# A four-layer recurrent stack on one core: weight preparation spread behind the first 64 RNN steps, initial states through the recurrence's own matmuls, vectors loaded as rows, and a hinted loop branch

## What is computed

```python
x = x + L0(x)   # RNN:  h_t = tanh(x_t @ Wx + b + h_(t-1) @ Wh),  h_0 = cond
x = x + L1(x)   # conv with 4 taps (weights: cond), 64 states: s = decay*s + dt*softplus(..)*u ; y = tanh(..)*s ; y @ Wo
x = x + L2(x)   # LSTM: A = x_t @ Wx + b + h @ Wh (512 x 2048), h_0 = cond, c_0 = 0
def L3(x, cond, base, w1, b1, w2, b2, ln_g, ln_b):
    ae = layernorm(cond) * ln_g + ln_b            # (4, 512)
    h  = gelu(ae @ w1 + b1)                       # (4, 512)
    xw = h @ w2 + b2                              # (4, 8192), w2 is 512 x 8192 (16 MB)
    x_a, x_b = split(xw)                          # each (4, 512, 8), rank 8
    layer = base + einsum('bdr,bkr->bdk', x_a, x_b)   # one 512 x 512 matrix per sequence
    return einsum('btc,bco->bto', x, layer)
x = x + L3(x)
```

## Time and profile before

| | |
|---|---|
| profiled execution, its time / its span | 4620.95 us / 4618.9 us |
| median of 3 runs | 4627.35 us |
| busy: PE, DVE, ACT, POOL (share of the span) | 80%, 80%, 33%, 28% |
| prologue, span start to body 0 | 210.6 us |
| first tanh of bodies 0, 1 and 2 | 213.35, 292.01, 373.49 us |
| mean granted TensorE clock, all of the span | 0.96 |

### The profile page before, as it was taken

How to read it: one execution, slowest core, us unless ns; L and a number is a source line. 1 busy time by engine, 2 the same in 40 slices (tenths; PEclk the granted TensorE clock), 3 DMA queues, 4 the chain that set the end, 5 groups by cost and what they waited for, 6 DMA issues and landing times.

```text
span 4618.9 us, 252593 instructions
## 1 busy us (share of the span) xinstructions
PE 3707.8 (80%) x106846; PEld 2997.8 (65%) x106846; DVE 3678.6 (80%) x20952; ACT 1530.7 (33%) x6667; POOL 1283.4 (28%) x4520
## 2 busy tenths in 40 slices
PE   4557888888888888888888888888888888888875
PEld 4246667676666666666666666666666766666653
DVE  5337888888888888888888888888888888888866
ACT  0013333333333333333333333333333333333321
...
DMA packets 28394, 64.27 MB, mean 14 GB/s; under 512 B 11068, under 2 KB 11708, under 8 KB 26120
## 3 DMA queue, kind: packets, MB, share of 16 engines
...
...
## 4 chain that ended last, share of the span: by engine, by line
DVE 39%; PE 33%; ACT 10%; POOL 8%; issue 7%; DMA 1%; SPq 1%; DVEq 0%; POOLq 0%; ACTq 0%
PE ps_lstm L898 29%; DVE lstm_sums L716 10%; DVE lstm_arg L722 6%; DVE lstm_h_scaled L745 4%; ACT lstm_gates_2c L491 4%; ACT lstm_tanh_c L496 3%; DVE lstm_gates_2c L733 3%; POOL stage L378 3%; DVE lstm_ig_fc L728 2%; POOL stage L379 2%; DVE lstm_h_parts L753 2%; DVE rnn_h_parts L817 2%; DVE lstm_h_parts L749 2%; DVE rnn_arg L781 2%; DVE lstm_o_scaled L737 2%
## 5 line engine op out<-in xcount | busy, mean ns | idle before, releaser
L898 PE MATMUL ps_lstm<-lstm_Wh_parts,lstm_h_parts 128*20 128x256 f16 x65536 | 2039.9, 277 | 660.4 <-DVE lstm_h_parts L753 615.5
L898 PEld LDWEIGHTS ps_lstm<-lstm_Wh_parts,lstm_h_parts 128*20 128x20 f16 x65536 | 1508.2, 92 | 1182.8 <-DVE lstm_h_parts L753 932.7
L716 DVE STREAM_TRANSPOSE lstm_sums<-ps_lstm 128x256 f32<-128x256 f32 x2048 | 913.0, 446 | 180.7 <-PE ps_lstm L898 135.3
L491 ACT ACTIVATE lstm_gates_2c<-lstm_arg 128x32 f32<-128x32 f32 x2048 | 470.9, 230 | 1660.8 <-DVE lstm_arg L722 1660.0
L353 POOL COPY lstm_sums<-lstm_in 128x32 f32<-128x32 f32 x2048 | 412.5, 211 | 1408.0 <-DVE lstm_arg L722 1394.2
L926 PE MATMUL ps_rnn<-rnn_Wh_parts,rnn_h_parts 128*20 128x128 f16 x32768 | 651.1, 222 | 73.6 <-DVE rnn_h_parts L819 71.0
L926 PEld LDWEIGHTS ps_rnn<-rnn_Wh_parts,rnn_h_parts 128*20 128x20 f16 x32768 | 552.9, 93 | 117.6 <-DVE rnn_h_parts L819 97.9
L722 DVE TENSOR_REDUCE lstm_arg<-lstm_sums 128x32 f32<-128x96 f32 x2048 | 535.6, 262 | 106.7 <-DVE lstm_o_scaled L737 0.6
L496 ACT ACTIVATE lstm_tanh_c<-lstm_gates_2c 128x8 f32<-128x8 f32 x2048 | 413.1, 202 | 392.5 <-DVE lstm_gates_2c L733 384.8
L516 ACT ACTIVATE rnn_h<-rnn_arg 128x16 f32<-128x16 f32 x1024 | 221.1, 216 | 929.6 <-DVE rnn_arg L781 929.6
L817 DVE TENSOR_SCALAR rnn_h_parts<-rnn_h 128x16 f16<-128x16 f32 x1024 | 237.7, 232 | 291.1 <-ACT rnn_h L516 291.1
(11 more groups left out here) (156 smaller groups left out, 3474.7 us busy)
## 6 DMA issues: line engine op xcount, KB each, us to landing
...
out<-out_rows SPq DMA_DIRECT2D x128, 64.0 KB, 1.9
...
```

The costliest lines, as they stand in the source:

```text
L491: A.activation(gate[h][:, 0:G, :].rearrange("p g q -> p (g q)"), arg[h][:, :, :].rearrange("p g n -> p (g n)"), ACT.Tanh, scale=gate_scale ...
L716: return mark(V.transpose(tr[h][s % 2][:, :, 0:QC], psL[h][:, 0:HW].rearrange("p (g c) -> p g c", c=QC)))
L898: ins = mm(psL[h][QC * j:QC * j + LO + NB, 0:HW], hls[:, k, :], whl[:, k, h, e, j, :], start=(k == 0 and e == 0), stop=(k == KB - 1 and e ...
```

## The change

The prologue keeps the RNN's weights, the layernorm and the first input chunk. The rest becomes pieces: `prepare(r)` is called behind each of the steps r = 0 to 63, which are the steps of bodies 0 and 1, on PE and DVE, with matching pieces in ACT's, POOL's and SP's bodies; the barrier is gone. The steps are: w1 at 1, gelu at 2, the maximum of the LSTM's weights in 8 pieces at 2 to 9, w2 in 16 pieces of 1 MB at 4 to 19 with four buffers, scales at 10 to 12, the split of the LSTM's weights in 16 pieces at 13 to 28 (ACT now scales them and makes one of the four parts), the LSTM's initial product at 17, 21, 25 and 29, the state layer's constants at 30, and the 16 products of the last layer at 34 to 49. `cond` enters both recurrences through their own product buffers (`psR`, `psL`) in fp32 with a scaled `cond_r`, `cond_l`. The additions of `b2` are four more matmuls per piece. Vectors are loaded as rows by 13 DMAs of ACT's queue and turned by PE. All loops carry a hint for their closing branch. The diff, cut to its core:

```diff
-W2C = 1024
+W2C = 512
+W2BUFS = 4
...
+W1_STEP = 1
+GELU_STEP = 2
+W2_STEP = 4
+LMAX_STEP = 2
+LMAX_W = 1024
+LMAX_N = KB * G * D // LMAX_W
+LSCALE_STEP = LMAX_STEP + LMAX_N
+LSPLIT_STEP = LSCALE_STEP + 3
+H0_STEPS = [LSPLIT_STEP + G * (k + 1) for k in range(KB)]
+SSM_PREP_STEP = H0_STEPS[-1] + 1
+LAYER_STEP = H0_STEPS[-1] + 5
...
-            with eng.Fori(FIRST_FULL, LAST_FULL, 2) as i:
+            with nc.Fori(FIRST_FULL, LAST_FULL, 2, engines=[eng.engine], hint_back_edge=True) as i:
...
 def _(sp):
+            sp.dma_start(whr32, rows(l0_Wh)).then_inc(d_rnnw, 16)
+            sp.dma_start(xrow[:, :], x_v[0]).then_inc(d_x0, 16)
+            sp.dma_start(wxr[:, :, :], rows(l0_Wx)).then_inc(d_rnnx, 16)
+            sp.dma_start(whl32, rows(l2_Wh)).then_inc(d_lstmw, 16)
+            sp.dma_start(w1s, rows(w1)).then_inc(d_w1, 16)
+            for q in range(W2BUFS - 1):
+                load_w2(q)
...
                 if w["l0_after"]:
                     sp.wait_ge(S["xT_mm"], 1)
                     sp.dma_start(xrow[:, :], x_v[i + 2]).then_inc(S["next_x_arrived"], 16)
+                if known == 0:
+                    sp.wait_ge(r_split, KB)
+                    sp.wait_ge(rnn_h0_mm, 1)
+                    for q in range(W2BUFS - 1, W2R):
+                        if q >= W2BUFS:
+                            sp.wait_ge(w2_mm, q - W2BUFS + 1)
+                        load_w2(q)
+                    sp.wait_ge(w2_mm, W2R)
+                    sp.dma_start(wxl[:, :, :], rows(l2_Wx)).then_inc(d_wx, 16)
...
+                if known == 1:
+                    sp.wait_ge(l_split, KB * G)
+                    sp.wait_ge(lstm_h0_mm, KB)
+                    sp.dma_start(baseI, rows(base)).then_inc(d_base, 16)
...
-            sp.wait_ge(q_pe, PE_X0)
+            sp.wait_ge(x0_mm, 1)
             sp.dma_start(xrow[:, :], x_v[1]).then_inc(x_arrived, 16)
...
 def _(pool):
+                    if known == 0 and s == LSCALE_STEP:
+                        pool.wait_ge(lmax_s, 1)
+                        Q.partition_all_reduce(wmaxa[:, 1:2], wmax[:, 1:2], P, RMAX).then_inc(lmax_all, 1)
...
 def _(act):
+                def low_rank_rows(q):
+                    act.wait_ge(w2_mm, q + 1)
+                    A.activation(xw[:, q // (W2R // 2), :, q % (W2R // 2), :],
+                                 (psB, psOut)[q % 2][:, 0:WQ].rearrange("p (d r) -> p r d", r=RANK), ACT.Copy).then_inc(xw_ready, 1)
+                def lstm_weights(u):
+                    k, g = u // G, u % G
+                    src = whl32[:, k, g * D:(g + 1) * D]
...
+                    A.activation(src, src, ACT.Identity, scale=lgate[:, g // (G - 1):g // (G - 1) + 1]).then_inc(l_src, 1)
+                    act.wait_ge(l_src, u + 1)
+                    A.activation(whl[:, k, 0, 0, :, g * HB * QC:(g + 1) * HB * QC]..., ACT.Copy).then_inc(l_hi0, 1)
...
 def _(vec):
+            def prepare(r):
...
+                if LMAX_STEP <= r < LMAX_STEP + LMAX_N:
+                    prep(V.tensor_reduce(lmax[:, u:u + 1], ...[:, LMAX_W * u:LMAX_W * (u + 1)], AX.X, ALU.max, ...))
...
+                if LSPLIT_STEP <= r < LSPLIT_STEP + KB * G:
+                    vec.wait_ge(l_src, u + 1)
+                    prep(V.tensor_copy(hi1, s4[:, 1]))
+                    V.tensor_tensor(lo1, s4[:, 1], hi1, ALU.subtract)
+                    vec.wait_ge(l_hi0, u + 1)
+                    V.tensor_tensor(lo0, s4[:, 0], hi0, ALU.subtract).then_inc(l_split, 1)
...
+                if LAYER_STEP < r <= LAYER_STEP + NB * KB:
+                    u = r - LAYER_STEP - 1
+                    vec.wait_ge(layer_mm, u + 1)
+                    V.tensor_tensor(layer[:, u // KB, u % KB, :], (psOut, psB)[u % 2][:, :], baseI[:, u % KB, :], ALU.add
+                                    ).then_inc(layer_ready, 1)
...
 def _(pe):
+                        if known == 0 and s == 0:
+                            ...
+                                    last = mm(psR[QC * j:QC * j + LO + NB, 0:RW], cond_r[:, k, :], w_, ...)
...
+                    if known in (0, 1):
+                        prepare(CT * known + s)
...
                     if w["l0"] and s == XT_STEP:
+                        if known == 0:
+                            pe.wait_ge(x_arrived, 16)
```

562 lines of the change are left out of this document (280 added, 282 removed).

## The result

The changed kernel takes **4484.35 us** (median of 4 runs, 4479.15 to 4501.56) where the kernel before, on the same chip, takes 4626.28 us (4 runs). The ratio is 0.9702, with a 95% interval of 0.9673 to 0.973. The forecast was 4427 us: the direction was right, and some 57 us of the expected gain are missing.

A forecast was written before the change was run, and what follows sets the result against it. It saw three places to gain: a 210.6 us prologue, 160 us of mostly idle engines in bodies 0 and 1, and 51 us of branches. 4620.95 - 155.8 - 44 = 4421, forecast 4427 us with the median's offset; range 4385 to 4485.

The forecast's parts named there:

- Start of body 0: Before step 0: load the RNN's weights, maximum, split and one input product, ending by 20 to 22 us.
- Step 1's tanh at 36.2 us: Second input chunk lands at 32.2 us behind 10.8 MiB, then turning and next tanh; bounds 28 and 45.
- Body 0, 91 us: Body 0, steps 1 to 31: summed step groups, including 1.8 us for two stalls; body 1's tanh at 127 us.
- Room plus the length of a piece: Body 0: a DVE piece of length D makes a step max(2.02, 1.30 + D) us; room is DVE's 0.73 us wait.
- Clock in body 0: TensorE at the high clock from step 4; at the low level, w2 steps 22 us longer in all.
- w2's loads and SP's 32 small DMAs at nothing: Body 0: both hidden behind steps; uncovered w2 loads up to 10 us, small DMAs a holdup over 1.0 us each.
- Body 1, 90.5 us: Body 1: 9 us added by last-layer products, `base` wait and additions; body 2's first tanh at 217.7 us.
- rival 2: First 64 steps stretch: low clock (+32), w2 loads (+10), x at 45 (+9); with all, 4478 us; chance 0.12.
- Hint, 44 us: Loop's closing branches: hint saves 3.7 us at each of 12, 44 us in all; bounded by 0 and 51 or 70.
- Rival 1: Loop branches: the hint does nothing, since instruction packets move in order; time 4471 us; chance 0.12.
- Rival 3: More comes back: fourth step goes with the branch (-26), pieces overlap better (-15); 4386 us; chance 0.15.
- A sign by which I had said that I would be wrong: Loop: wrong if the distance at the branches stays at 8 us or other steps of the loop grow.

The follow-up runs named there:

- slot 0: Each engine's loop head placed at the start of a 256-instruction fetch block; with the hint, 4449.91 us on the changed kernel, 4586.41 us on the kernel before.
- the fastest version: Changed kernel plus 128-row layer products, early `base` load, second chunk ahead of the LSTM's weights, loop heads at fetch-block starts: 4431.51 us, ratio 0.9596.

## Why the prediction went wrong, step by step

- **Start of body 0** was right: 23.4 us, "before 25".
- **Step 1's tanh at 36.2 us** was too early by 7.7. The step that failed is the queue's: "SP issues that behind 10.8 MiB" took the chunk to follow those bytes at once, at no cost of its own. The bytes about kept to the rates (11.1 MB by 33 us), but SP's issue was slow (17.30 us for three), and the chunk was issued only at 32.05 us and took 8.1 us more. It lies within the bound of 45.
- **Body 0, 91 us**, measured 92.5. The sums of the groups held: steps 2 to 9 20.7, measured 21.9; 13 to 19 22.8, measured 22.8; 20 to 28 23.7, measured 22.9; step 30 5.7 and 5.70. Room plus the length of a piece is a sound price where nothing else stands in a step (2.33 us in steps 2 to 6 for 2.45, 2.52 in most of 20 to 28 for 2.63). In the w2 steps the agreement is partly luck: 13 to 16 took 3.94, 3.17, 4.27 and 3.40 us and 17 to 19 only 2.68, where I had 3.25 for each, and the two longest of them hold waits of PE for its issue, which the chain through ACT had no part in. The largest miss is step 10, 7.36 for 2.8. PE in order of time, in its w2 piece:

```profile
66.98 0.83 PE L916 MATMUL ps_lstm_in_b<-lstm_Wx,hmT 128*32 128x128 f32 x22
70.39 0.69 PE L916 MATMUL ps_lstm_in_b<-lstm_Wx,hmT 128*32 128x128 f32 x10 [2.59 <-issue]
71.01 0.65 PE L920 MATMUL ps_lstm_in_b<-b_rows,ident 64*32 64x128 f32 x8
71.59 2.07 PE L1084 MATMUL ps_lstm_in_a<-stage,rnn_Wx 128*128 128x128 f32 x8
```

  PE waited 2.59 us for its own issue amid one product, and the next product ran at the low clock. The term that failed is the 1.8 us for two stalls: there were four, 7.35 us, at the blocks' ends (steps 7, 10, 13 and 15), and shorter steps elsewhere made up for it.
- **Clock in body 0**, taken as high from step 4 on: right up to the end of w2, and wrong behind it, where it had no price. The table by stretch of the changed kernel (columns as above) has it:

```profile
90.00:105.00 15.00, 9.17 (x340) 6.11 (x328) 10.18 (x39) 7.29 (x20) 1.72 (x7) 1.00 0.48 157
105.00:120.00 15.00, 7.83 (x216) 4.93 (x208) 11.01 (x42) 7.47 (x18) 1.66 (x7) 0.55 0.54 204
```

  From 105 us on the clock is 0.55, but DVE's split pieces bound those steps, as their 22.9 us for 23.7 suggest.

- **w2's loads and SP's 32 small DMAs at nothing**: right. The small DMAs took 26 us and ended at 127 us, and the last tanh of body 0 stands at 134.3.
- **Body 1, 90.5 us**: wrong, 111.7. The step is "About 0.9 us at the high clock": the piece was priced at the high clock throughout, because four contiguous products had been enough to raise it in the earlier trace rows. These were 128 rows deep and the new ones are 8. The text had a price for the low clock (10 us in body 1, as part of rival 2), half of what it cost. With 128 rows body 1 took 94.6 us, 17.1 less. The second term, 2 us for `base`, was 6.1 (8.15 for a step of 2.03), since it is issued 10 us before it lands. Taking that wait away gained 3 us with 8 rows, as the next step took up the rest, and 6.1 with 128. Together that is 23.2 us, more than the miss of 21.2: body 1 then takes 88.5 us, 2 less than forecast.
- **Hint, 44 us**: wrong, 16 by the medians. I took "the idle 3.22 us and a part of the slow issue behind it" as one thing that a hint cures wherever the code lies. Measured, on the kernel before the hint alone gave nothing; on the changed one it gave 23 to 27 us against the form without the hint, whose loop is 16 us longer than before; and with slot 0 it gave 38 us on the kernel before. PE's idle time without a releaser, added up over the 12 turns of the loop that end in a branch back, shows it: 42.3 us before, 43.3 in the change without the hint, 30.8 with it, 0 with hint and slot 0. Rival 1 (the hint does nothing, 0.12) came true on the kernel before alone. Its reason, instructions that come in order in packets, fits the waits at the blocks' ends, but the branches did get shorter.

The miss adds up: 7.7 + 1.5 + 21.2 + 27.5 = 58, against 4484.35 - 4427 = 57. The median lies at the very top of the range, and the ratio of 0.9702 just beyond it (4485 of 4627.35 is 0.9692), since most of rival 1 and part of rival 2 came together, which I had left out of it. Rival 3, more coming back at the branches, needed slot 0, and even the fastest version stands at 4431.5. A sign by which I had said that I would be wrong came: other steps of the loop grew, and the branches took 7.0 us in the mean in place of 4 to 5.
